# A GRU step whose elementwise part is written as prefix scans of 64 and 48 elements

## What is computed

```python
def step(h, xt):
    xr_t, xz_t, xn_t = xt
    r = jax.nn.sigmoid(xr_t + h @ w_hr.T + b_hr)
    z = jax.nn.sigmoid(xz_t + h @ w_hz.T + b_hz)
    n = jnp.tanh(xn_t + r * (h @ w_hn.T + b_hn))
    h_new = (1.0 - z) * n + z * h
    return (h_new, h_new)
```

## Time and profile before

| | before |
|---|---|
| time, median of 3 runs | 1625.4 us |
| lowest and highest run | 1619.39 and 1628.22 us |
| the profiled execution's own time | 1626.28 us |
| its span, first to last instruction | 1624.5 us |
| mean granted TensorE clock | 0.664 of full speed |
| TensorE matmuls busy (modelled ends) | 1371.2 us, 84% |
| TensorE weight loads busy | 1033.9 us, 64% |
| VectorE busy | 1129.3 us, 70% |
| ScalarE busy | 683.8 us, 42% |
| GpSimd busy | 432.6 us, 27% |

### The profile page before, as it was taken

The page is one execution under the profiler, slowest core; times in us unless marked ns, Lnnn a source line. Parts: engine busy times, 40 slices in busy tenths (PEclk is TensorE's granted clock), DMA queues, the critical chain, the costliest instruction groups (busy, mean ns, idle before and its releaser), DMA issues. The chain is left out here.

```text
span 1624.5 us, 65673 instructions
## 1 busy us (share of the span) xinstructions
PE 1371.2 (84%) x27355; PEld 1033.9 (64%) x27370; DVE 1129.3 (70%) x5594; ACT 683.8 (42%) x2475; POOL 432.6 (27%) x818
## 2 busy tenths in 40 slices
PE   5888888888888888888888887479999999999886
PEld 4677777777777777777777775345555556555443
DVE  5667777777777777777777776565676766676485
ACT  3332223222222222222222222126777767777764
POOL 2001111111111111111111112444435635522364
PEclk6555555555555555555555555569999999999998
DMA  5200000000000000000000000086735744742001
GB/s 120 30 4 5 5 6 5 5 7 5 5 7 5 5 7 5 5 6 5 5 6 5 5 7 5 29 159 104 92 61 94 101 68 77 116 58 32 1 15 39
DMA packets 68941, 53.70 MB, mean 33 GB/s; under 512 B 12686, under 2 KB 68390, under 8 KB 68646
## 3 DMA queue, kind: packets, MB, share of 16 engines
q1 hardware_dynamic: 66470, 49.32, 18.8%
q10 hardware_dynamic: 2176, 0.20, 0.1%
HBM read 31.84 MB, written 15.47 MB: 29 GB/s over the span
## 5 line engine op out<-in xcount | busy, mean ns | idle before, releaser
L735 PE MATMUL PS<-GB,W 128*128 128x8 f16 x18432 | 576.1, 168 | 158.2 <-DVE GB L1045 141.5
L735 PEld LDWEIGHTS PS<-GB,W 128*128 128x128 f16 x18432 | 532.9, 104 | 266.9 <-DVE GB L1045 261.2
L2387 DVE TENSOR_REDUCE MX<-PS 128x1 f32<-128x512 f32 (+3 forms) x352 | 219.9, 635 | 118.0 <-PE PS L1846 115.1
L939 ACT ACTIVATE tr<-PS 128x16 f32<-128x16 f32 x512 | 93.7, 183 | 487.3 <-PE PS L735 487.2
L2125 ACT ACTIVATE PT<-PS 128x512 f32<-128x512 f32 (+1 forms) x352 | 193.3, 566 | 120.2 <-PE PS L1862 115.8
L1031 DVE SCALAR_TENSOR_TENSOR u_<-tr,PS 128x16 f32<-128x16 f32 x512 | 87.5, 171 | 126.4 <-PE PS L735 114.3
L941 ACT ACTIVATE tz<-PS 128x16 f32<-128x16 f32 x512 | 93.7, 183 | 193.8 <-PE PS L735 193.8
L689 POOL TENSOR_TENSOR rt<-mv,eps 128x1 f32<-128x1 f32 x96 | 18.2, 189 | 541.7 <-DVE mv L1056 541.7
L1843 PE MATMUL PS<-KS,QS 99*128 99x256 bf16 (+3 forms) x512 | 134.5, 315 | 11.3 <-DVE MX L2387 10.0
L1038 DVE SCALAR_TENSOR_TENSOR zg<-tz,HR 128x16 f32<-128x16 f32 x512 | 90.1, 176 | 77.0 <-ACT tz L941 64.6
L1859 PE MATMUL PS<-QS,KS 102*128 102x256 bf16 (+3 forms) x512 | 130.7, 306 | 6.3 <-ACT PT L2125 5.7
(11 more groups left out here) (393 smaller groups left out, 2502.4 us busy)
## 6 DMA issues: line engine op xcount, KB each, us to landing
QS<-q_parts SPq DMA_DIRECT2D x90, 128.0 KB, 11.2
KS<-k_parts SPq DMA_DIRECT2D x90, 128.0 KB, 13.5
q_parts<-PQ SPq DMA_DIRECT2D x16, 384.0 KB, 11.1
k_parts<-PK SPq DMA_DIRECT2D x16, 384.0 KB, 3.2
X<-XM SPq DMA_DIRECT2D x32, 64.0 KB
out_dram<-X SPq DMA_DIRECT2D x8, 256.0 KB, 2.3
XM<-in_L_attn_x_dram SPq DMA_DIRECT2D x16, 80.0 KB
s_hh<-in_L_attn_w_hh_dram SPq DMA_DIRECT2D x1, 768.0 KB, 5.5
```

The lines of the kernel that those rows point to most:

```text
L735: return pe.matmul(bank[:, p, at:at + B], W[:, kc, w:w + P], state[:, part, kc, :], start=False, stop=True, skip_group_check=True)
L939: act.activation(as_states(tr), now(pR), ACT.Tanh, scale=gate_scale).then_inc(hn_tr.sem, 1)
L2387: dve.tensor_reduce(MX[:, g % 2, heads[0]:heads[-1] + 1, NT - 1 - it], p_x[:, k % 2, 0:len(heads) * w].rearrange("p (a w) -> p a w", w=w), ...
```

## The change

- The candidate's pre-activations stand in PSUM in groups of four columns per state element (`candidate`), filled so that one prefix scan, state = state * `RQ` + column, started at zero, gives the candidate's argument at the fourth place. `RQ` is (0, 1, tr, 1) for each element; ScalarE writes `tr` into its third place. This scan of 64 elements takes the place of `u_` and `v`.
- For that, `W1` times low and high state are one product with 32 moving columns (`candidate_w1`, the pair repeated by the access pattern), and `W2` times high state one with 16 columns which writes the second and fourth places (`candidate_w2`). The candidate has 8 products instead of 12, a step 32 instead of 36. The biases go to the second and fourth places and the input's share to the third.
- The order of products is: 8 of the reset gate, 4 `candidate_w2`, 2 of the update gate, wait for the low state, 4 of the reset gate (`r_ps`), 4 `candidate_w1`, the other 10 of the update gate.
- ScalarE writes the negated `tz` into `ZT` (0, -tz, 1) by a negative scale, and the candidate twice into `NT3`. VectorE writes (-tz - 1) * `HG` into the third place of `NT3`, where `HG` is -0.5 times the fp32 state. A scan of 48 elements over `ZT` and `NT3` gives the fp16 state (`GQ`, candidate, partial sum, state), and a second one the fp32 state (`HR`). `zg`, `zn` and the two old state operations go.
- The low state is written into the second place of `GQ`; `GQ` holds two steps and is the moving operand, read at a stride of three. A new operation makes `HG` behind it.
- ScalarE copies each step's low and high state from `GQ` into the history `GB` (`keep`), behind the candidate's tanh of the next step; the output projection waits for these copies (`states_kept`).
- Set-up: the constant places of `RQ` and `ZT` are written once, and one more scale (`minus_scale`) is made.

```diff
...
-            HR = sb(ctx, "HR", [P, 2, NSTEP])
+            HR = sb(ctx, "HR", [P, NSTEP, 3])
+            GQ = sb(ctx, "GQ", [P, 2, HC, B, 3], FP16)
             GB = sb(ctx, "GB", [P, RG, 2, HC, GS, B], FP16)
-            tr = sb(ctx, "tr", [P, NSTEP])
-            tz = sb(ctx, "tz", [P, NSTEP])
-            u_ = sb(ctx, "u_", [P, NSTEP])
-            zg = sb(ctx, "zg", [P, NSTEP])
-            zn = sb(ctx, "zn", [P, NSTEP])
+            RQ = sb(ctx, "RQ", [P, NSTEP, 4])
+            ZT = sb(ctx, "ZT", [P, NSTEP, 3])
+            NT3 = sb(ctx, "NT3", [P, NSTEP, 3])
+            HG = sb(ctx, "HG", [P, NSTEP])
+            LOW, HIGH = 1, 2
...
+            def candidate(p):
+                return pN[:, p, 0:4 * U * NSTEP].rearrange("p (u c b i) -> p u c b i", u=U, c=HC, i=4)
+
             def v_of(p):
-                return pN[:, p, 2 * U * NSTEP:2 * U * NSTEP + NSTEP]
-
-            def n_of(p):
-                return pN[:, p, 2 * U * NSTEP + NSTEP:2 * U * NSTEP + 2 * NSTEP]
-
+                return pN[:, p, 4 * U * NSTEP:4 * U * NSTEP + 4 * NSTEP]
...
                 def product(gate, p, k, state, mc, kc, W, part):
                     bank, g = gates[gate]
                     w = (HC * g + mc) * P
                     at = (mc * U + k) * B
-                    return pe.matmul(bank[:, p, at:at + B], W[:, kc, w:w + P], state[:, part, kc, :],
+                    return pe.matmul(bank[:, p, at:at + B], W[:, kc, w:w + P], state[:, kc, :, part],
                                      start=False, stop=True, skip_group_check=True)
 
+                def candidate_w2(p, k, state, mc, kc):
+                    w = (HC * 2 + mc) * P
+                    return pe.matmul(candidate(p)[:, k, mc, :, 1:4:2], W2[:, kc, w:w + P],
+                                     state[:, kc, :, HIGH].unsqueeze(2).to_broadcast([P, B, 2]),
+                                     start=False, stop=True, skip_group_check=True)
+
+                def candidate_w1(p, k, state, mc, kc):
+                    w = (HC * 2 + mc) * P
+                    return pe.matmul(candidate(p)[:, k, mc, :, :].rearrange("p b (o i) -> p b o i", o=2), W1[:, kc, w:w + P],
+                                     state[:, kc, :, LOW:HIGH + 1].unsqueeze(2).to_broadcast([P, B, 2, 2]),
+                                     start=False, stop=True, skip_group_check=True)
...
                 def inject(gates_at, p, rows, start):
-                    for bank, first, bias, chunk in gates_at:
+                    for bank, which, bias, chunk in gates_at:
                         for mc in range(HC):
-                            o = bank[:, p, first + mc * U * B:first + (mc + 1) * U * B]
+                            if which is None:
+                                o = bank[:, p, mc * U * B:(mc + 1) * U * B]
+                            else:
+                                o = candidate(p)[:, :, mc, :, which].rearrange("p u b i -> p u (b i)")
                             if bias is not None:
-                                pe.matmul(o, brow[:, (bias + mc) * P:(bias + mc + 1) * P], ones3[:, :],
+                                n = 2 * U * B if which == HIGHS else U * B
+                                pe.matmul(o, brow[:, (bias + mc) * P:(bias + mc + 1) * P],
+                                          ones3[:, 0:n] if which is None else ones3[:, 0:n].rearrange("p (u n) -> p u n", u=U),
                                           start=start and mc == 0, stop=False, skip_group_check=True)
                             if chunk is not None:
                                 w = slice((chunk + mc) * P, (chunk + mc + 1) * P)
                                 for V, Y in ((V1, Y1), (V2, Y1), (V1, Y2)):
-                                    pe.matmul(o, V[:, w], Y[:, rows],
+                                    y = Y[:, rows]
+                                    pe.matmul(o, V[:, w], y if which is None else y.rearrange("p (u b) -> p u b", u=U),
                                               start=False, stop=False, skip_group_check=True)
                         start = False
...
-                XN_AT = U * NSTEP
-                r_in = [(pR, 0, 0, 0)]
-                z_in = [(pZ, 0, 2, 2)]
-                n_in = [(pN, 0, 4, None), (pN, XN_AT, 6, None)]
-                xn_in = [(pN, XN_AT, None, 4)]
+                HIGHS, THIRD = slice(1, 4, 2), slice(2, 3)
+                r_in = [(pR, None, 0, 0)]
+                z_in = [(pZ, None, 2, 2)]
+                n_in = [(pN, HIGHS, 4, None), (pN, THIRD, 6, None)]
+                xn_in = [(pN, THIRD, None, 4)]
...
+                    state = GQ[:, 1 - s % 2, :, :, :]
                     pe.wait_ge(g1_ready.sem, n)
                     for w in by_g1:
-                        product("r", p, k, state, *w, 0)
-                    for w in by_g1[:3]:
-                        product("n", p, k, state, *w, 0)
+                        product("r", p, k, state, *w, HIGH)
+                    for w in tiles:
+                        candidate_w2(p, k, state, *w)
+                    for w in tiles[:2]:
+                        product("z", p, k, state, *w, W2, HIGH)
                     pe.wait_ge(g2_ready.sem, n)
-                    for w in by_g2:
-                        last = product("r", p, k, state, *w, 1)
+                    for w in tiles:
+                        last = product("r", p, k, state, *w, W1, LOW)
                     last.then_inc(r_ps.sem, 1)
-                    for w in by_g1[3:]:
-                        product("n", p, k, state, *w, 0)
-                    for w in by_g2:
-                        last = product("n", p, k, state, *w, 1)
+                    for w in tiles:
+                        last = candidate_w1(p, k, state, *w)
                     last.then_inc(hn_tr.sem, 1)
-                    for w in by_g1:
-                        product("z", p, k, state, *w, 0)
-                    for w in by_g2:
-                        last = product("z", p, k, state, *w, 1)
+                    for w in tiles[2:]:
+                        product("z", p, k, state, *w, W2, HIGH)
+                    for part in (HIGH, LOW):
+                        for w in tiles:
+                            last = product("z", p, k, state, *w, W1, part)
                     last.then_inc(z_ps.sem, 1)
...
-                            pe.wait_ge(g2_ready.sem, GS * (u + 1) + 1 if isinstance(u, int) else pe.snap(u * GS + (GS + 1)))
+                            pe.wait_ge(states_kept.sem, GS * (u + 1) if isinstance(u, int) else pe.snap(u * GS + GS))
...
+                def keep(n, ring, s):
+                    act.wait_ge(g2_ready.sem, n + 1)
+                    act.activation(GB[:, ring, :, :, s, :].rearrange("p i c b -> p c b i"), GQ[:, s % 2, :, :, LOW:HIGH + 1],
+                                   ACT.Copy).then_inc(states_kept.sem, 1)
...
                     act.wait_ge(r_ps.sem, n)
-                    act.activation(as_states(tr), now(pR), ACT.Tanh, scale=gate_scale).then_inc(hn_tr.sem, 1)
+                    act.activation(member(RQ, 2), now(pR), ACT.Tanh, scale=gate_scale).then_inc(hn_tr.sem, 1)
                     act.wait_ge(z_ps.sem, n)
-                    act.activation(as_states(tz), now(pZ), ACT.Tanh, scale=gate_scale).then_inc(tz_ready.sem, 1)
+                    act.activation(member(ZT, 1), now(pZ), ACT.Tanh, scale=minus_scale).then_inc(tz_ready.sem, 1)
                     act.wait_ge(v_ready.sem, n)
-                    act.activation(n_of(p), v_of(p), ACT.Tanh, scale=n_scale).then_inc(n_ready.sem, 1)
+                    act.activation(NT3[:, :, 0:2],
+                                   v_of(p).rearrange("p (n i) -> p n i", i=4)[:, :, 3:4].to_broadcast([P, NSTEP, 2]),
+                                   ACT.Tanh, scale=n_scale).then_inc(n_and_old.sem, 1)
+                    if not (isinstance(first, int) and first + s == 0):
+                        keep(first + s, *((ring, s - 1) if s else ((ring - 1) % RG, GS - 1)))
...
+                    one_row = lambda x: x.rearrange("p n i -> p (n i)")
+                    hn_and_xn = candidate(p)[:, k, :, :, :].rearrange("p c b i -> p (c b i)")
+                    states = GQ[:, s % 2, :, :, :]
 
                     dve.wait_ge(hn_tr.sem, n2)
-                    dve.scalar_tensor_tensor(by_chunk(u_[:, :]), by_chunk(tr[:, :]), 1.0, hn,
-                                             ALU.add, ALU.mult).then_inc(u_ready.sem, 1)
-
-                    dve.wait_ge(u_ready.sem, n)
-                    dve.tensor_tensor(by_chunk(v_of(p)), by_chunk(u_[:, :]), xn, ALU.add).then_inc(v_ready.sem, 1)
+                    dve.tensor_tensor_scan(v_of(p), one_row(RQ[:, :, :]), hn_and_xn, 0.0,
+                                           ALU.mult, ALU.add).then_inc(v_ready.sem, 1)
 
                     dve.wait_ge(tz_ready.sem, n)
-                    dve.scalar_tensor_tensor(zg[:, :], tz[:, :], 1.0, before, ALU.add, ALU.mult).then_inc(zg_ready.sem, 1)
-
```

(19 more changed lines are left out.)

46 lines of the change are left out of this document (27 added, 19 removed).

## The result

The changed kernel takes 1585.4 us (median of 4 runs, 1583.0 to 1588.1); the kernel before, beside it, 1625.4 (median of 3 runs, 1619.4 to 1628.2). The ratio is 0.976, 95% interval 0.973 to 0.979. It is faster, inside the range, and some 15 us slower than the 1570 forecast. One execution of the kernel before (3240.6 us) and, further down, one of the kernel with the state scans alone (1786.5 us) were far slower than the rest and stand in no comparison.

The account below looks back on a forecast made before the run. The prediction took a chain of waits in the 512-step recurrence, 1.90 us a step, as the bound; 512 x (1.784 - 1.90) = -59 and +4 on 1626.3 us gave 1571, rounded to 1570, range 1540 to 1650.

Parts of the forecast that it names:

- What bounds the kernel: Recurrence of 512 steps: no engine saturated, a chain of waits sets the step at 1.90 us.
- Scans: VectorE scans: 2.04 ns per element, so 293 ns for 64 elements and 258 ns for 48.
- the reciprocal: VectorE row at 5.8 ns per further element, taken as upper bound for a scan's element time; about 1868 us.
- The rivals with a fast and a slow scan: VectorE scan at 1.02 ns an element: 1546 us, chance 0.11; above two element times, 1644 at three: chance 0.14.
- Order of products: TensorE: first tanh 0.68 after first load, update gate's 1.05; low part arrives after 14 products, no gap, no slack.
- Spread outputs: Rival on TensorE: candidate products writing every second PSUM column take 0.054 instead of 0.027; step 1.89, 1626 us; chance 0.09.
- Old part as the bound: Next state scan's two inputs come within 0.02; the old part ends last at 1.47, giving a period of 1.78.
- Small things: Half state's VectorE operation fills two of 16 slots, +4 us; second wait and copy cost nothing; set-up under 1 us.
- The second wait and the copy: Old part's `half_ready` wait costs nothing, at most 36 us; ScalarE history copy of 0.19 fits, without cover up to 97.
- The sum: 512 x (1.784 - 1.90) = -59, and +4, on 1626.3 us: 1571, rounded to 1570.
- The likeliest case: The forecast itself: 1570 us, own range 1555 to 1612, chance 0.63.
- The clock: Rival: wider products raise TensorE's granted clock, loads at half of 0.027, down to about 1400 us; chance 0.03.

Follow-up runs that it names:

- state scans alone: Changed kernel with the candidate as before (36 products, sum and product as two operations, no scan of 64): ratio to before 1.007.
- the run with 96: Changed kernel with its second state scan (fp32 state) over 96 elements instead of 48: ratio to before 1.006.
- 16 ahead: Changed kernel with 16 instead of 14 products ahead of the wait for the low part: ratio to before 0.986.
- results side by side: Changed kernel with four small results (three tanhs, old part) written side by side into tiles of their own; scans read constants: ratio to before 0.973.
- candidate scan alone: Kernel before with only merged products (32) and the scan of 64; state kept elementwise, 11 products ahead of the low part: ratio to before 0.974.
- 12 products ahead: Changed kernel with 12 instead of 14 products ahead of the wait for the low part: ratio to before 0.992.

## Why the prediction was right, and where it was off

- **What bounds the kernel.** Right. No engine is saturated, before or after, and every edit that touched a chain moved the step by the length that the chain says: +0.097 for a scan 0.099 longer, +0.051 for a gap of 0.050, +0.031 for 0.051 more on the chain with some 0.02 of room.
- **Scans.** The term with the largest uncertainty came out almost exact: 295 and 258 ns for the forecast's 293 and 258, 2.06 ns for each further element by the run with 96. Only the second state scan, with its result in fp32, is shorter than forecast, 233 ns. Twice 1.02, the middle between an ordinary element and one of the running maximum, was the right size, but the choice of it was a guess from two dependent operations, which no run tests; the reciprocal was no more than a bound. The Trainium skill, "DVE: opcode table, instruction layouts, handler registers and perf-mode slots", section 6, has the scan at half throughput; the trace agrees, with 2.06 ns beside the 0.94 of an ordinary further element. The rivals with a fast and a slow scan fall with these rows.
- **Order of products.** Right: 0.68 to the first tanh, 1.05 to 1.06 to the update gate's, no gap at the low part and no slack.
- **Spread outputs.** This rival did not happen: the spread products follow each other at 0.027 like the others. The Trainium skill, "Advanced Engine Details and Errata", section "Memory Cachelines", has any non-contiguous pattern slow matmuls significantly; with 16 columns at every second place, and 32 merged ones, no row here shows that.
- **Old part as the bound.** Right, by some 0.020 (16 ahead) for a forecast 0.021. Its forecast length was 0.026 short, 511 x 0.026 = 13 us: the step that failed is the cost of its answers. I took 0.22 from the update gate's tanh to the old part and 0.20 from there to the scan, the figures of results that lie side by side; they are 0.23 and 0.21. Averaged over the quiet steps, from the scan to the first load, to the update gate's tanh, to the old part and to the next scan, it is 0.311 + 1.059 + 0.224 + 0.216 = 1.810, and with the results side by side 0.310 + 1.058 + 0.218 + 0.211 = 1.797, where the forecast had 0.31 + 1.05 + 0.22 + 0.20. Half of the 0.026, 0.013, is thus the spaced writing, which the forecast had not priced at all. The other half is in the main the scan's start after the old part, 0.211 for 0.20 with the results side by side too, and a start of the update gate's tanh read 0.006 too early from one step (1.16; the mean over the quiet steps of before is 1.166).
- **Small things.** This term was mis-sized, and its mechanism was wrong. I put +4 us on the full slots of VectorE; in the slot of the earlier trace rows the quiet steps last 1.807, no longer than in most others. Two other slots of the 16 have quiet steps of 1.823 and 1.828, 1.2 us in all; in the second the old part takes 0.205 beside a small operation of GpSimd, and neither was tried. What came instead, in another slot, is GpSimd's addition: 26 steps of 0.30, some 8 us, which one moved wait took away. That the sum's +4 stands for half of it is luck. The step that failed is that the old part's new start was worked out within the step but not laid against GpSimd's timeline, where it moved from 0.33 after the addition's start to 0.01. That would have shown it: the high part's maximum of 652, beside a GpSimd operation of 2.16 us, hinted that VectorE can be held (though it ended before that operation did), and `zg` had escaped the addition by little. In four kernels (before, changed, candidate scan alone, results side by side) the held operation ends at a fixed distance after the addition, whenever it began: the old part 0.03 after it for starts of 0.01 (0.48 long), 0.13 (0.36, in the candidate scan alone) and 0.25 (0.24), the state scan 0.11 after it for starts of 0.20. An operation with one input in SBUF was not held: `v` of the kernel before, which takes its other input from PSUM, began up to 0.01 after the addition 28 times and took its usual 178 ns. The Trainium skill, "SBUF — State Buffer", section "Who interferes with whom", says that a VectorE instruction with two SBUF inputs and a GpSimd instruction that reads SBUF contend, and that the order of issue decides which one waits; the trace agrees. The other order is shown by the results side by side: in 26 of 29 meetings the old part begins between 0.01 ahead of the addition and 0.00 behind it by the record, takes its usual 0.18, and the addition takes 0.49 to 0.50 instead of 0.46. The changed kernel has one such meeting too, with the old part less than 0.01 behind by the record.
- **The second wait and the copy.** The copy is free, as taken, by the run without it. So is the second wait: from the update gate's tanh to the old part it is 0.218 with two waits and the results side by side, and 0.215 in the kernel before with one (means over the quiet steps). The copy's size was off (0.335 for 0.19), its cover was not.
- **The sum.** Forecast for the recurrence: 974.1 - 59 + 4 = 919. Measured: 935.6, 17 more. The quiet step fell by 0.091 (1.901 to 1.810) instead of 0.116, 511 x 0.025 = 13 us; the other steps rose by 10.9 - 2.7 = 8 us instead of 4. The likeliest case was the right one, and its own range (1555 to 1612) held the time.
- **The clock.** The rival was wrong in its mechanism, not only in its chance; see the end.

## What to carry to other kernels

Where a loop is bound by a chain of short operations, ask of each part of a change whether it shortens the chain that ends last: here one scan that replaced two dependent operations, together with the four products fewer that let the update gate come earlier, brought all of the gain, and a second that looked alike brought none, because its longer duration moved a later result. When an operation gets new operands or a new place, look at what GpSimd does at that moment, for a meeting of a few tenths of a microsecond on the path costs the same as a whole extra operation. And a scan is priced by its elements, here at 2.06 ns against 0.94 for an ordinary element, so pad it no further than needed.

## What the runs showed of the hardware that was not expected

The granted clock does not matter to this recurrence. It was 0.50 from 300 to 600 us in the changed kernel, and 1.00 in the profiles without copies and with 12 products ahead:

```profile
300.00:600.00 300.00, 255.23 (x6731) 221.54 (x6729) 243.56 (x1283) 108.19 (x534) 51.42 (x122) 1.00 0.02 6
```

TensorE was busy 255 us of the 300 at either level, the loads were 0.027 apart at either, and the quiet step was 1.809 and 1.810. Runs of the kernel before on one chip agree: 1620.5 to 1627.2 us at a mean clock of 0.66 (seven runs), 1623.6 to 1630.0 at 0.98 (four). Products of 8 to 32 columns behind a 128 x 128 load are here paced by something that both levels share, and what that is no run shows; a gain from a higher clock was not to be had.

A copy on ScalarE of 32 fp16 elements that lie in pairs takes 335 ns, where a tanh of 32 results in fp32 takes 198. The two differ in type, in pattern and in where they read, and which of these it is was not tried.
